# Local transformer: the score products cut into quarters between other TensorE work, and six output heads between the two mixtures

## The reference, cut to what matters

```
q, k, v = split(shift_tokens(x) @ Wqkv)          # v of the windows is folded into m below
q = rotate(l2norm(q) * q_scale)
k = rotate(l2norm(k) * k_scale)
bk2, bv2 = look(bk), look(bv)                    # each window of 32 tokens sees itself and the one before
sim = einsum('bhwie,bhwje->bhwij', bq, bk2) * 8
attn = softmax(where(mask, -max, sim))
x = x + einsum('bhwij,bhwje->bhwie', attn, bv2) @ Wo
...
x = x + (a * gelu(gate)) @ W2 + b2               # a, gate = split(layernorm(shift_tokens(x)) @ W1 + b1)
```

## Time and profile before

| | us |
|---|---|
| median of 3 runs | 5482.02 (5480.84 to 5488.46) |
| the profiled execution | 5474.09 |
| its span in the trace | 5472.3 |
| PE busy | 4684.0 (86%) |
| DVE, ACT, POOL busy | 3691.4, 2818.3, 2814.0 |
| granted TensorE clock, mean | 0.938 |

### The profile page before, as it was taken

One profiled execution on the slowest core, in us unless ns is written; L12 is line 12 of the kernel. 1 busy time (PEld: TensorE's weight loads), 2 busy tenths in 40 slices (PEclk: granted clock), 3 DMA queues, 4 the chain that ended last, 5 costly groups with the idle time before them and its releaser, 6 DMA issues. The chain is left out here.

```text
span 5472.3 us, 143416 instructions
## 1 busy us (share of the span) xinstructions
PE 4684.0 (86%) x57103; PEld 3323.3 (61%) x57103; DVE 3691.4 (67%) x8589; ACT 2818.3 (52%) x6208; POOL 2814.0 (51%) x3349
## 2 busy tenths in 40 slices
PE   7699999999999999999999999965374999945896
PEld 3366666666666666666666666644263767623665
DVE  7777777777777777777777777747724656667443
ACT  2266666666666666666666565631022666641342
POOL 4476666767667667667776676711022333311000
PEclk9899999999999999999999999987587999967898
DMA  0211111111111111111111110000211000010102
GB/s 21 71 29 25 25 34 36 25 25 33 31 28 24 33 33 29 25 35 29 29 25 35 24 27 17 21 19 8 68 50 33 1 2 1 2 24 9 29 27 59
DMA packets 312164, 150.62 MB, mean 28 GB/s; under 512 B 146143, under 2 KB 301003, under 8 KB 311243
## 3 DMA queue, kind: packets, MB, share of 16 engines
q1 hardware_dynamic: 309451, 137.20, 10.4%
q0 software_dynamic: 2048, 4.20, 0.3%
HBM read 101.10 MB, written 27.41 MB: 23 GB/s over the span
## 5 line engine op out<-in xcount | busy, mean ns | idle before, releaser
L1435 POOL TENSOR_TENSOR loc_a<-loc_a,loc_b 128x512 f32<-128x512 f32 x768 | 979.0, 1278 | 236.5 <-DVE loc_b L1511 236.0
L1123 PE MATMUL psum<-loc_wqk,loc_xt 128*128 128x512 f32 x1536 | 824.8, 619 | 15.1 <-DVE loc_b L1511 5.9
L1186 PE MATMUL psum<-loc_m,xn_rows 128*128 128x128 f32 x6144 | 823.5, 277 | 5.2 <-DVE y_rows L1543 3.0
L1307 ACT ACTIVATE loc_sq<-psum 128x512 f32<-128x512 f32 x768 | 455.3, 593 | 684.0 <-PE psum L1123 683.5
L1460 POOL TENSOR_TENSOR loc_a<-loc_a,loc_rn 128x512 f32<-128x512 f32 x768 | 787.0, 1049 | 0.1
L1186 PEld LDWEIGHTS psum<-loc_m,xn_rows 128*128 128x128 f32 x6144 | 753.7, 193 | 48.3 <-issue 45.6
L1467 POOL TENSOR_TENSOR xn_cols<-xn_cols,loc_rec 128x512 f32<-128x512 f32 x384 | 394.0, 1047 | 686.0 <-DVE loc_rec L1538 685.6
L1507 DVE TENSOR_TENSOR loc_a<-psum,loc_rope 128x512 f32<-128x512 f32 x768 | 523.3, 681 | 330.3 <-ACT loc_sq L1307 318.6
L1344 ACT COPY xn_rows<-psum 128x512 f32<-128x512 f32 x768 | 411.9, 588 | 219.1 <-PE psum L1174 215.4
L1511 DVE TENSOR_TENSOR loc_b<-psum,loc_rope 128x512 f32<-128x512 f32 x768 | 520.6, 678 | 0.0
L1515 DVE TENSOR_REDUCE loc_n<-loc_sq 128x8 f32<-128x512 f32 x768 | 516.9, 673 | 0.0
(11 more groups left out here) (370 smaller groups left out, 8490.1 us busy)
## 6 DMA issues: line engine op xcount, KB each, us to landing
loc_x<-loc_shifted SPq DMA_DIRECT2D x192, 256.0 KB, 4.0
loc_shifted<-y_rows SPq DMA_DIRECT2D x144, 64.0 KB
loc_wqk<-in_L_ffn_Wqkv SPq DMA_DIRECT2D x24, 256.0 KB, 3.8
x_rows<-y_rows SPq DMA_DIRECT2D x96, 64.0 KB
x_rows<-y_rows SPq DMA_DIRECT2D x96, 63.5 KB
moe_w<-in_L_ffn_W SPq DMA_DIRECT2D x16, 256.0 KB, 4.7
l3a_qk<-l3a_rot SPq DMA_DIRECT2D x16, 256.0 KB, 2.1
grp_w<-in_L_ffn_W SPq DMA_DIRECT2D x16, 256.0 KB, 4.2
```

Source lines behind the costliest of these rows:

```text
L1123: nc.tensor.matmul(ring("p", i, unit), xt[:, b % 2, t * P:(t + 1) * P], wqk[:, unit * 512:(unit + 1) * 512], start=True, stop=True).then_i ...
L1186: last = nc.tensor.matmul(y_bank[:, 0:P], u[:, i % 2, h // 2, h % 2, :], m[:, h, :], start=(h == 0), stop=(h == HEADS - 1))
L1307: nc.scalar.activation(sq[:, g % 2, :], ring("p", i, unit), ACT.Square).then_inc(sem["squared"], 1)
L1435: nc.gpsimd.tensor_tensor(part, part, b_[:, g % 2, :], ALU.add).then_inc(sem["added"], 1)
```

## The change

`scores` is split into `mask_scores`, the eight mask products with the wait for the banks, and `scores(i, pairs)`, which does the products of some pairs of heads; the wait for k stands before the first of them, and `scored` is raised behind the last. `project_out(i, heads)` takes any range of heads. On TensorE the mask now goes ahead of the first half of the probabilities, and the four quarters of two pairs each stand behind it, behind projection 3, behind the second half of the probabilities and behind heads 8 and 9. Heads 10 to 15 come between the mixtures. The second mixture goes ahead of hidden piece 1. On ACT the exponentials move behind the copies of rows, of the first mixture and of x, and the second mixed copy goes ahead of the second gelu. No operation is added or left out.

```diff
-                def scores(i):
-                    b, t = i // TPB, i % TPB
-                    pe.wait_ge(sem["copied"], copied_at["k", i, 1])
+                def mask_scores(i):
+                    t = i % TPB
                     if i >= 1:
                         pe.wait_ge(sem["shifted"], 2 * i)
...
+                def scores(i, pairs):
+                    b, t = i // TPB, i % TPB
+                    if pairs.start == 0:
+                        pe.wait_ge(sem["copied"], copied_at["k", i, 1])
+                    for j in pairs:
...
-                    last.then_inc(sem["scored"], 1)
+                    if pairs.stop == PAIRS:
+                        last.then_inc(sem["scored"], 1)
...
                     if now(0):
                         project(n, 2)
+                    if now(2):
+                        mask_scores(n - 2)
                     if now(3):
                         turn_probs(n - 3, 0)
                     if now(2):
-                        scores(n - 2)
+                        scores(n - 2, range(0, 2))
                     if now(0):
                         project(n, 3)
+                    if now(2):
+                        scores(n - 2, range(2, 4))
                     if now(3):
                         turn_probs(n - 3, 1)
+                    if now(2):
+                        scores(n - 2, range(4, 6))
                     if now(4):
-                        project_out(n - 4, 2)
+                        project_out(n - 4, range(8, 10))
+                    if now(2):
+                        scores(n - 2, range(6, 8))
...
                     if now(4):
-                        project_out(n - 4, 3)
+                        project_out(n - 4, range(10, 16))
+                    if now(3):
+                        mix(n - 3, 1)
                     if group_at(n, 12) is not None:
                         hidden(group_at(n, 12), 1)
-                    if now(3):
-                        mix(n - 3, 1)
...
                         copy_turned("p", n - 3, 1)
-                    if now(2):
-                        exps(n - 2, 0)
-                        exps(n - 2, 1)
...
                         copy_x((n + 1) // 2)
+                    if now(2):
+                        exps(n - 2, 0)
+                        exps(n - 2, 1)
                     if group_at(n, 12) is not None:
                         gelu(group_at(n, 12), 0)
-                        gelu(group_at(n, 12), 1)
                     if now(3):
                         copy_mixed(n - 3, 1)
+                    if group_at(n, 12) is not None:
+                        gelu(group_at(n, 12), 1)
```

More of the change, by code:

```diff
@@ L1144, in scores @@
                                              skip_group_check=True)
-                    for j in range(PAIRS):
+                def scores(i, pairs):
[3 more added lines that the diff above has]
+                    for j in pairs:
                         for w in range(WPT):
@@ L1176, in mix, with project_out @@
                     last.then_inc(sem["u_done"], 1)
-                def project_out(i, part):
-                    if part == 0:
+                def project_out(i, heads):
+                    if heads.start == 0:
                         pe.wait_ge(sem["u_copied"], 4 * (i + 1))
@@ L1184, in project_out @@
                             pe.wait_ge(sem["stored"], i)
-                    for h in range(4 * part, 4 * part + 4):
+                    for h in heads:
                         last = nc.tensor.matmul(y_bank[:, 0:P], u[:, i % 2, h // 2, h % 2, :], m[:, h, :], start=(h == 0),
                                                 stop=(h == HEADS - 1))
-                    if part == 3:
+                    if heads.stop == HEADS:
                         last.then_inc(sem["y_done"], 1)
@@ L1249, in _ @@
                     if now(4):
-                        project_out(n - 4, 0)
+                        project_out(n - 4, range(0, 4))
                     if now(2):
@@ L1253, in _ @@
                     if now(4):
-                        project_out(n - 4, 1)
+                        project_out(n - 4, range(4, 8))
                     if now(2):
```

## The result

| | before | after |
|---|---|---|
| median of 4 runs each | 5481.43 (5471.74 to 5488.46) | 5589.09 (5585.87 to 5595.07) |
| ratio, 95% interval | | 1.0191 (1.0175 to 1.0207) |
| span of the profiled execution | 5472.3 | 5593.3 |
| PE busy | 4684.0 (86%) | 4832.7 (86%) |
| granted TensorE clock, mean | 0.938 | 0.935 |

What follows compares the result with a forecast made beforehand. TensorE was taken as the bound. Terms +110 - 58 + 20 - 85 gave -13 us, from 5474.09 to 5461 for the profiled execution; against the runs' median 5482.02 the forecast was 5469 us, range 5400 to 5540.

Steps and rivals of the forecast that it cites:

- The stalls: TensorE's instruction stalls in the scores: quarters spread the dense matmuls, some 93 us fall to 8; -85 us (0 to -93).
- the rival in which they stay: Score stalls move elsewhere or do not depend on density; +72 us, 5554 us, chance 0.08.
- the step where row and page spoke against each other: Stalls term: the page's "mostly hidden" block crossings leave nothing to win, sum +72; profile rows show 54 gaps, 82.1 us.
- The list of TensorE: Scores in quarters, third projection to output heads: more array switches make it +0.57 us a step, +110 us over 192 tiles.
- The sum that was forecast as 4.97: TensorE's rebuilt list from third projection to output heads: 4.97 us against 4.50 before, +0.47 a step.
- The rivals of slow quarters (0.46): Score quarters keep the section's slow pace of 9.7 ns a matmul; sum +57 us, 5539 us, chance 0.15.
- cheap ones (0.34): Array switches cheaper than charged: fourth quarter into mixture free, quarters 0.34 us; -59 us, 5423 us, chance 0.22.
- Six heads: Six heads between the mixtures cover ACT's mixed copy; with the hidden pieces' new order, TensorE's waits shrink; -58 us.
- ACT: ACT's exponentials moved later delay the second mixed copy (+13 us) and the first gelu (+7); +20 us (0 to 40).
- the forecast sum of -13: Quarters +110, heads -58, ACT's later exponentials +20 and stalls -85 together give -13 us.
- DVE: Later scores delay DVE's maxima, subtractions and rotation, but the next step hides this with over 1 us spare; no cost.
- a rival in which ACT's later exponentials hold up every step: ACT's later exponentials cost another 0.1 to 0.2 us every step; +30 us, 5500 us, inside the range, no separate chance.

Runs made afterwards that it cites:

- e2: The changed kernel with mask and scores whole again in their old place, heads and ACT's order as changed; 5492.38 us, ratio 1.0019.
- e3: The kernel before with only the scores cut into two halves around the fourth projection; 5556.64 us, ratio 1.0136.
- e4: e2 with the scores in halves around the fourth projection; 5497.54 us, ratio 1.0032.
- e5: e4 with the second half of the scores directly before the first mixture and DVE's fourth rotation before its shift; 5392.05 us, ratio 0.9835.
- e1: The changed kernel with DVE's fourth rotation ahead of the subtraction of score maxima; 5451.11 us, ratio 0.9949.
- e8: e1 with ACT's exponentials back ahead of the copies of rows, mixture and x; 5883.41 us, ratio 1.0739.
- e9: The changed kernel with DVE's fourth rotation before the shift only in steps with hidden pieces, one in four; 5489.47 us, ratio 1.0011.
- e6: The kernel before with DVE's fourth rotation before the shift and nothing else; 6388.07 us, ratio 1.1658.

## Why the prediction was wrong

**The stalls: right.** Forecast: 82.1 us of idle for "issue" fall to under 15. Measured 0.2. Whole scores have 82.1 and 70.0 us (before, e2), halves around one projection 13.0 and 13.7 (e3, e4), quarters 0.2. In e5, whose halves have more between them, they are 0.7. So the stalls go with how densely the section uses up instructions, and the rival in which they stay is out. That what runs out is the fetched instructions is inferred from the packet of the earlier trace rows; "issue" alone does not say so. This term is the step where row and page spoke against each other. The page "Runtime: NRT & Kernel Launch" of the Trainium skill, Instruction fetch mechanics, calls the crossing of blocks "mostly hidden". The 54 gaps of before say otherwise for 256 instructions in 1.4 us, and with less dense work the page's word holds.

**The list of TensorE: right.** Over all steps, the median quarter is 0.384 (0.37 forecast), the third projection into the mask 0.954 (0.95), mask to transposes 0.34 (0.33), transposes between quarters 0.586 (0.58), the fourth projection 1.056 (1.05), heads between 0.642 (0.64). The sum that was forecast as 4.97 is 5.06, which is 17 us more over the 192 tiles, most of it in the quarters. The passage from the last score matmul to the mixture takes 0.146, against 0.15 charged. That agrees with "Mode switching requires drain" of the Trainium skill's page "TensorEngine Tiling (Array Packing)", also between two part-array shapes. The rivals of slow quarters (0.46) and of cheap ones (0.34) are both out.

**Six heads: right, with a condition.** The waits of the earlier trace rows went, from 36.9 us to about 1. e2 shows that this needs the quarters in the place left behind.

**ACT: charged too high, and wrong in kind.** I took the move of the exponentials as a price of 20 us. In e1 the transposes of q in the step behind the rows' step start 0.08 us later than in before (1.06 for 0.98 from the second projection's start), 4 us over 45 steps where I charged 13, and hidden piece 1 comes 0.02 later behind the second mixture, where I charged 0.15. Left where they were, the exponentials cost 432 us (e8). e1, which holds every term of the forecast and not the wait for DVE, comes out at -32 us against the forecast sum of -13.

**DVE: the step that failed.** "So DVE hides the delay, with over 1 us to spare": the sum has no term for what is queued on DVE behind the late scores, and the runs show 138 us in its place. I added up the shift and the rotation and compared their end with the next step's second projection. That reader of the bank was fine. Two others were not looked at:
- The ring has two banks, and the GLU's pieces use it too. In every fourth step the value product of hidden piece 0 needs the bank of projection 3 some 2 us after the scores' end (2099.58, when the mixture starts, to about 2101.6, the piece's start and 0.9 for the gate), not over 4 us. Measured 2.0 us a time, 100 us by e9.
- In every fourth step DVE does 2.69 us of row work before its first rotation, and TensorE's third projection needs the bank that this rotation reads. The step whose start I compared with comes one later and has no such work. That both engines "have a quarter of their time free" is an average over steps that differ. Measured 38 us.

Together 138 us (e1), which is more than the whole error of 120 us (5589.09 against 5469); the other terms came out some 19 us better than forecast, as e1 shows.

I had named a rival in which ACT's later exponentials hold up every step, priced at 30 us and inside the range, and a new wait of TensorE for DVE as a sign of being wrong, without a price. The changed kernel's loss is that new wait, in two steps of four, and over four times as large as the rival. By cycles of four steps, start to start and without stalls: before 67.93 us, after 72.10, e1 69.28. The list's own growth is 69.28 - 67.93 = 1.35, 48 x 1.35 = 65 us, less 93 for the stalls with their restarts: 28 faster, as e1 measures (32). With the waits it is 48 x 4.17 - 93 = 107 slower, as measured (107.7).

**What stays open.** Why the stalls with halves still come 25 to 32 times and at which place of the stream they fall was not tried by moving single instructions. Nor was the row work on DVE moved, so the second wait's cause rests on the timeline and on e9, which leaves it standing by itself.

## What to carry to other kernels

When a producer moves later, look on the waiting engine at everything queued behind that wait, and list *all* readers and writers of the buffers which that queue releases, in each kind of step, not only the usual one. An in-order queue has to be reordered together with the one that feeds it: the same swap of two calls was worth -138 us with the new order of TensorE and +905 with the old. To break up a dense run of small matmuls one cut is nearly enough here (82.1 us of stalls fall to 13 with one projection in it, to 0.7 with more), and every further cut costs some 0.2 us each time.

## What the hardware showed that was not expected

The clock answered to waits. In e6 TensorE waits some 3 us for the mixed copy. Timeline of PE in e6:

```profile
2025.08 1.76 PE L1174 MATMUL psum<-xn_cols,loc_x 64*128 64x256 f32 x8 [3.23 <-ACT xn_rows L1344]
2026.77 2.07 PE L1123 MATMUL psum<-loc_wqk,loc_xt 128*128 128x512 f32 x2
```

and the windows view of the same kernel:

```profile
1300.00:2300.00 1000.00, 834.59 (x10436) 580.19 (x10435) 605.59 (x1106) 489.32 (x938) 561.99 (x688) 0.92 0.10 24
...
2026.00:2027.00 1.00, 1.00 (x5) 0.35 (x4) 1.00 (x2) 0.13 (x1) 1.00 (x2) 0.50 0.00 0
```

From start to start the mixture behind the wait takes 1.69 us (2025.08 to 2026.77), where the last one in the earlier trace rows takes 1.07, and the projection behind it 1.86 (2026.77 to 2028.63) for the 0.96 between 2020.16 and 2021.12 in before. The granted clock is 0.50 in the microsecond from 2026, the 1.2 GHz level, and 0.92 over the 1000 us, where before has 1.00. So some 550 us of added waits came with 905 us of added time. The mean granted clock of the whole execution was 0.885 over 6377.3 us and 0.938 over 5472.3: 733 us were taken away by it and 339 in before, 394 more. That is enough for the rest, though part of it fell into the waits themselves, and it was not tried by itself. In the changed kernel, whose longest such wait is 1.8 us, the granted clock was 0.99 over the same stretch. There the idle time of the two waits is 106.7 us and their removal gave 138; the clock, 1.00 in e1, can hold part of the difference.

The second: between two part-array shapes the switch from the last score matmul to the mixture takes 0.146 us, as much as the 0.15 from the last score to the projection in the earlier trace rows (which then pays another 0.10 before its second matmul), while the mask (64 x 512, bf16) passes into the scores of the same 64*32 shape at no cost that shows.
